# Two recurrent layers re-timed slot by slot, and an attention loop with fewer, larger transfers

## The chip, the cores and the metric

The program runs on one core of a Trainium2 chip. It is one launch, and the time is the device time of that launch in microseconds, the median of the runs. Five engines work side by side: TensorE (PE, with PEld for its weight loads), VectorE (DVE), ScalarE (ACT), GpSimd (POOL) and SyncE (SP), which here issues every transfer. Each has its own instruction stream, and they meet at semaphores.

## The reference, cut to what matters

Two blocks, each with modulated layer norms, a mixer and a feed-forward part with rounding to four bits. The mixer of the first block is attention with relative positions, 8 batches of 1024 tokens and 16 heads of 16 columns; that of the second is two recurrent layers of 512 channels and 16 states:

```python
# block 0: attention, per batch and head
scores = Q @ K.T * scale + take(Q @ pos_key.T, clip(rel)) + take(K @ pos_query.T, clip(-rel)).T
ctx = softmax(scores) @ V

# block 1: one recurrent layer (twice)
conv = causal_conv4(xc) + cb;  u = silu(conv)
dt, Bm, Cm = split(u @ xp_w.T)
dt = softplus(dt @ dt_w.T + dt_b)              # 512 channels
h_t = exp(dt_t * A) * h_(t-1) + (dt_t * u_t) * B_t     # 16 states a channel
y_t = sum_n h_t[n] * C_t[n]
y = (y + u * Dskip) * silu(z)
out = layer_norm(y @ out_w.T) * ln_w + ln_b + residual
```

## The kernel before, in words

**Attention** (`attention_loop`). There are 128 heads (8 batches by 16). A head has 8 tiles of 128 queries; each engine runs a loop over pairs of heads, with the 16 tiles of a pair written out. Index `n` is the head, `i` the tile, `m = 8n + i`. In iteration `i` TensorE computes the scores of the next tile (`scores`), two position tables of the same tile index of the next head (`table`, one for each side), turns the probabilities of this tile (`turn`) and multiplies those of the tile before with the values (`context`). ScalarE copies each table from PSUM to `tab` (L966) and takes the exponent (L971); VectorE adds the near positions and takes the row maximum (L1018, L1020).

The tables are shifted row by row through memory: SP stores each `tab[:, e, :]` to `table_dram` (`store_table`, L784), and `load_skew` (L793) reads it back with a row pitch one shorter, into `skew`. A head has four parts of two tiles (`PARTS`), and each part is read with four transfers after its stores have landed. `scores` of tile 0 waits for part 0, tile 1 for part 1, tile 3 for part 2 and tile 5 for part 3. SP's program order is written out by hand in `head`: T stands for the stores of one tile, S for the reads of a part, O for `load_opnd` (three transfers: q, kl, kr, L771), E for `load_eopnd` (two transfers, L775). Over one head it is O E T0 S3 val T1 T2 S0 ctx T3 T4 S1 T5 T6 S2 T7. S0 to S2 are those of the next head, S3 the last part of this one. `eopnd` holds the first 96 rows of q and kl once more, for `table` alone.

**Recurrent layers** (`mamba_layer`, `mb_` names). A layer has 16 items of 512 tokens. An item has 64 slots: slot `s` is channel group `c = s // 16` and state `n = s % 16`. In each slot ScalarE makes `dA` (exp, ring of 2, L2198), GpSimd makes `bx = dtu * B` (ring of 4, L1921), VectorE scans `hs` (L2016) and multiplies the state of the slot before with C (`g`, L1976), and TensorE adds `g` into `y_ps` (L2159). In 18 of the 64 slots (`TIMES_C_POOL`, slots 3, 7, 10, 14, ... 60, 63) GpSimd makes `g` instead (L1928), three slots later. The rest of the next item's and the last item's work is hung on fixed slots by the `AT_` constants (L1588 to L1606). ScalarE may be at most two slots ahead of the scan and GpSimd four.

The work that the change moves: for each of the four channel groups a softplus, of six ScalarE steps in one slot (`log_steps`, L2177 to L2184), one VectorE step (`softplus_sum`, L2002) and three GpSimd steps in one slot (`make_dtu`: `rest` L1934, `dt` L1937, `dtu` L1940); the centring of the output rows on ScalarE (`center`, L2188, four instructions), their multiplication with the norm weight and addition of its bias on VectorE (L2040, L2044; in the second layer also L2049 and L2053) and the residual on GpSimd (L1952); in the first layer the same for the input rows (L2065, L2068). `silu` of `u` stands in slot 45 on ScalarE, `silu` of `z` in slot 12, each with a table load on both sides. The loops run over pairs of items, an item with `u = 1` first.

## Time and profile before

| | us |
|---|---|
| median of 3 runs | 10254.26 (10250.23 to 10259.6) |
| profiled execution, its own time | 10262.97 |
| span of the profiled execution | 10261.3 |
| attention loop | about 660 to 4070 |
| recurrent layers | about 4980 to 7270 and 7330 to 9600 |

The page divides the span by engine: PE 8391.0 us (82%), DVE 8398.0 (82%), ACT 5633.4 (55%), POOL 4948.9 (48%), and the one transfer queue 44.7%. These are means over stages with different limits, so each stage is to be read by itself.

### The profile page before, as it was taken

The page shows a single profiled execution, that of the slowest core. Times are in us where ns is not written, and L with a number is a line of the kernel's source. Part 1 is how long each engine was busy: PE and PEld are TensorE (multiplying, and loading weights), DVE is VectorE, ACT ScalarE, POOL GpSimd, SP SyncE. Part 2 cuts the span into 40 slices and gives each one's busy share as a digit, 9 for nine tenths or more (in the row PEclk, how much of TensorE's full clock was granted, in tenths as well). Part 3 has the DMA queues.
Part 4 walks back from the last instruction along what each step waited for, and adds up shares of the span by engine and source line. Part 5 has one row for each costly group of instructions (what it writes and reads, how often), then busy time and mean ns, then how long its engine had stood idle before and what let it go on. Part 6 is the DMA issues. An engine that isn't in the chain of part 4 may idle for free. (4 is left out here: it accounts for less than half of the span.)

```text
span 10261.3 us, 177062 instructions
## 1 busy us (share of the span) xinstructions
PE 8391.0 (82%) x48396; PEld 4841.9 (47%) x48396; DVE 8398.0 (82%) x13204; ACT 5633.4 (55%) x9153; POOL 4948.9 (48%) x4685
## 2 busy tenths in 40 slices
PE   4569899989988888499688888888688888887599
PEld 2236666666666666366333333333233333333366
DVE  4558888888888887699588888888688888888799
ACT  1237777777777776133365555555455555555233
POOL 0000000000000000088488888888598888888487
PEclk7779999999999999699898998898899999999799
DMA  5578888888888888311111111111122221122111
GB/s 178 204 234 281 277 278 279 279 279 278 277 279 277 277 278 261 111 43 42 61 74 76 76 68 55 68 74 75 51 80 84 84 84 71 62 81 80 45 43 40
DMA packets 1218155, 1498.79 MB, mean 146 GB/s; under 512 B 101997, under 2 KB 1073277, under 8 KB 1185000
## 3 DMA queue, kind: packets, MB, share of 16 engines
q1 hardware_dynamic: 1217832, 1495.78, 44.7%
q14 instruction: 279, 2.29, 0.1%
q8 instruction: 44, 0.72, 0.0%
HBM read 932.33 MB, written 564.60 MB: 146 GB/s over the span
## 5 line engine op out<-in xcount | busy, mean ns | idle before, releaser
L2159 PE MATMUL mb_y_ps<-mb_g,ident 128*128 128x512 f32 x4096 | 2227.9, 654 | 589.9 <-DVE mb_g L1976 356.3
L1921 POOL TENSOR_TENSOR mb_bx<-mb_dtu,mb_bc 128x512 f32<-128x512 f32 x2048 | 2569.3, 1282 | 132.7 <-DVE mb_hs L2016 78.6
L2198 ACT ACTIVATE mb_dA<-mb_dt,mb_a_neg 128x512 f32<-128x512 f32 x2048 | 1403.7, 689 | 1854.9 <-DVE mb_hs L2016 1181.4
L1355 POOL MEMSET f_magic<- 128x1 f32 x2 | 0.2, 98 | 3842.8 <-POOLq L127 3842.8
L2159 PEld LDWEIGHTS mb_y_ps<-mb_g,ident 128*128 128x128 f32 x4096 | 789.3, 204 | 1782.9 <-issue 755.4
L966 ACT ACTIVATE at_tab<-at_e_ps 128x384 f32<-128x384 f32 x2064 | 1011.8, 490 | 968.4 <-PE at_e_ps L883 967.4
L1020 DVE TENSOR_REDUCE at_nmax<-at_s_ps 128x1 f32<-128x1024 f32 x1025 | 1255.2, 1225 | 35.2
L899 PE MATMUL at_pT_ps<-ident,at_probs 128*128 128x128 f32 x8192 | 1115.7, 280 | 140.3 <-ACT at_probs L971 131.8
L971 ACT ACTIVATE at_probs<-at_s_ps,at_nmax 128x1024 f32<-128x1024 f32 x1025 | 1140.6, 1113 | 96.2 <-DVE at_nmax L1020 77.0
L899 PEld LDWEIGHTS at_pT_ps<-ident,at_probs 128*128 128x128 f32 x8192 | 920.0, 142 | 403.3 <-ACT at_probs L971 378.1
L2016 DVE TENSOR_TENSOR_SCAN mb_hs<-mb_dA,mb_carry,mb_bx 128x512 f32<-128x512 f32 x736 | 927.7, 1280 | 204.8 <-POOL mb_bx L1921 117.2
L1976 DVE TENSOR_TENSOR mb_g<-mb_hs,mb_bc 128x512 f32<-128x512 f32 x1472 | 994.0, 675 | 69.9 <-PE mb_y_ps L2159 68.6
L2016 DVE TENSOR_TENSOR_SCAN mb_hs<-mb_dA,mb_bx 128x512 f32<-128x512 f32 x736 | 893.6, 1223 | 165.0 <-ACT mb_dA L2198 96.1
L866 PE MATMUL at_s_ps<-at_opnd 105*128 105x512 bf16 (+3 forms) x2818 | 808.8, 327 | 201.9 <-DMA at_skew<-at_tables 199.2
L1018 DVE TENSOR_TENSOR at_s_ps<-at_s_ps,at_skew 128x384 f32<-128x384 f32 (+1 forms) x1025 | 541.2, 528 | 495.6 <-PE at_s_ps L870 375.1
L1928 POOL TENSOR_TENSOR mb_g<-mb_hs_sb,mb_bc 128x512 f32<-128x512 f32 x576 | 736.5, 1279 | 312.6 <-DVE mb_hs_sb L2016 180.2
L1025 DVE COPY at_probsT<-at_pT_ps 128x512 f32<-128x512 f32 x1024 | 697.0, 681 | 0.0
L918 PE MATMUL at_c_ps<-at_probsT,at_val 128*32 128x128 f32 x16384 | 663.9, 280 | 1.6 <-ACT at_probsT L978 1.6
L870 PE MATMUL at_s_ps<-ident,at_skew 128*128 128x128 f32 x2818 | 612.9, 275 | 0.0
L2092 PE MATMUL mb_ring<-mb_xc,mb_diag 128*128 128x512 f32 x1024 | 526.8, 600 | 41.6 <-ACT mb_u L2249 39.0
L918 PEld LDWEIGHTS at_c_ps<-at_probsT,at_val 128*32 128x32 f32 x16384 | 387.4, 109 | 214.6 <-issue 203.9
L866 PEld LDWEIGHTS at_s_ps<-at_opnd 105*128 105x128 bf16 x2818 | 242.8, 98 | 435.2 <-DMA at_skew<-at_tables 223.9
(236 smaller groups left out, 14473.1 us busy)
## 6 DMA issues: line engine op xcount, KB each, us to landing
at_tables<-at_tab SPq DMA_DIRECT2D x2064, 192.0 KB, 3.5
at_skew<-at_tables SPq DMA_DIRECT2D x1030, 256.0 KB, 3.1
mb_bc<-mb_bc_rows SPq DMA_DIRECT2D x256, 1024.0 KB, 6.4
at_skew<-at_tables SPq DMA_DIRECT2D x773, 128.0 KB, 3.5
at_opnd<-at_q_st SPq DMA_DIRECT2D x129, 210.0 KB, 3.4
at_opnd<-at_kl_st SPq DMA_DIRECT2D x129, 210.0 KB, 3.9
at_opnd<-at_kr_st SPq DMA_DIRECT2D x129, 210.0 KB, 5.2
at_eopnd<-at_q_st SPq DMA_DIRECT2D x130, 192.0 KB, 4.3
```

The lines of the kernel that those rows point to most:

```text
L866: mm = nc.tensor.matmul(s_ps[:, b, a * P:z * P], opnd[:, u, 0, q], opnd[:, u, side, a * P:z * P], start=True, stop=(len(near) == 0))
L899: mm = nc.tensor.transpose(pT_ps[:, hb, k * P:(k + 1) * P], probs[:, i % 2, c:c + P], ident[:, :])
L918: mm = nc.tensor.matmul(c_ps[lane * VW:(lane + 1) * VW, q:q + P], val[:, h.u, k + lane, :], probsT[:, i0 % 2, (k + lane) * P:(k + lane + 1 ...
L966: nc.scalar.activation(tab[:, e, :], e_ps[:, 0:BAND], ACT.Copy).then_inc(s_tab, 1)
L971: nc.scalar.activation(probs[:, i % 2, :], s_ps[:, i % 2, :], ACT.Exp, bias=nmax[:, i % 2:i % 2 + 1], scale=1.0).then_inc(s_exp, 1)
L1020: nc.vector.tensor_reduce(nmax[:, b:b + 1], s_ps[:, b, :], axis=AX.X, op=ALU.max, negate=True).then_inc(s_max, 1)
L1921: pool.tensor_tensor(bx[:, s % RINGS, :], dtu[:, c, :], bc[:, 0, n, :], ALU.mult).then_inc(s_bx, 1)
L1928: pool.tensor_tensor(g[:, s1 % RINGS, :], state(s1), bc[:, 1, s1 % STATE, :], ALU.mult).then_inc(s_gp, 1)
L1976: nc.vector.tensor_tensor(g[:, s1 % RINGS, :], state(s1), bc[:, 1, n, :], ALU.mult).then_inc(s_g, 1)
L2016: nc.vector.tensor_tensor_scan(state(s), dA[:, s % DA_RING, :], bx[:, s % RINGS, :], initial=carry[:, s:s + 1] if k.u else 0.0, op0=ALU.mu ...
L2159: nc.tensor.matmul(y_ps[:, c % 2, :], ident[:, :], g[:, s1 % RINGS, :], start=False, stop=(n == STATE - 1)).then_inc(s_y, 1)
L2198: nc.scalar.activation(dA[:, s % DA_RING, :], dt[:, c, :], ACT.Exp, scale=a_neg[:, c, n:n + 1]).then_inc(s_dA, 1)
```

## The change

In attention `eopnd` is gone: `table` reads the first 96 rows of `opnd`, each of whose three transfers now has its own semaphores, and `opnd` of head n+2 is loaded in iteration 6 of head n. The two table stores of a tile become one. The order on SP is now T0 S3 T1 T2 val ctx S0 T3 T4 S1 T5 O T6 S2 T7.

In the recurrent layers the softplus is split over two slots on ScalarE and three on GpSimd, the centring over two slots, and the norm steps, the residual and some others move to other slots.

```diff
-        eopnd = sb("eopnd", [ROWS, 2, 2, T], BF16)
...
-                    sp.dma_start(opnd[:, u, k, :], st[bass.ds(n, 1), :, :].rearrange("a r t -> (a r) t")).then_inc(s_op[u], 16)
-
-            def load_eopnd(n, u):
-                for k, st in enumerate((q_st, kl_st)):
-                    sp.dma_start(eopnd[:, u, k, :], st[bass.ds(n, 1), 0:ROWS, :].rearrange("a r t -> (a r) t")).then_inc(s_eop[u], 16)
+                    sp.dma_start(opnd[:, u, k, :],
+                                 st[bass.ds(n, 1), :, :].rearrange("a r t -> (a r) t")).then_inc(s_op[k][u], 16)
...
-            def store_table(n1, u1, e):
-                ge(sp, s_tab, n1 * NE + e + 1)
-                part = e // 2 // (TT // len(PARTS))
-                sp.dma_start(table_dram[u1, e % 2, e // 2, 0:P, SPAN:SPAN + BAND], tab[:, e, :]).then_inc(s_tw[part], 16)
+            def store_tables(n1, u1, t):
+                ge(sp, s_tab, n1 * NE + 2 * t + 2)
+                part = [t < z for _, z in PARTS].index(True)
+                sp.dma_start(table_dram[u1, :, t, 0:P, SPAN:SPAN + BAND].rearrange("s p u -> p s u"),
+                             tab[:, 2 * t:2 * t + 2, :]).then_inc(s_tw[part], 16)
...
-                load_opnd(n + 1, 1 - u)
-                ge(sp, s_E, (n + 1) * NE)
-                load_eopnd(n + 2, u)
                 for i in range(TT):
-                    for e in range(2 * i, 2 * i + 2):
-                        store_table(n + 1, 1 - u, e)
                     for part, (_, z) in enumerate(PARTS):
-                        if z - 1 + LAG - 1 == i + 1:
+                        if z + 1 == i:
                             load_skew(n + 1, 1 - u, part)
-                        if z - 1 + LAG - 1 == i + 1 + TT:
+                        if z + 1 == i + TT:
                             load_skew(n, u, part)
-                    if i == 0:
+                    if i == TT - 2:
+                        ge(sp, s_S, n * TT + TT)
+                        load_opnd(n + 2, u)
+                    store_tables(n + 1, 1 - u, i)
+                    if i == 2:
                         ge(sp, s_pv, n * TT)
                         load_val(n + 1, 1 - u)
...
-                if e == 0:
-                    ge(pe, s_eop[u1], h.j * 32 + 32)
+                if e < 2:
+                    ge(pe, s_op[e][u1], h.j * 16 + 16)
...
-AT_DTK, AT_DTK_ACT = (52, 2, 15, 32), (58, 8, 21, 38)
-AT_DTK_DVE, AT_DTK_POOL = (59, 9, 22, 39), (63, 13, 26, 43)
+AT_DTK, AT_DTK_ACT = (52, 2, 15, 32), (56, 8, 21, 38)
+AT_DTK_DVE, AT_DTK_POOL = (58, 11, 23, 40), (59, 12, 24, 41)
...
-AT_ONORM = 26
-AT_RES = 44
-AT_OCENTER, AT_OSCALE = 34, 37
-AT_HCENTER, AT_HSCALE = 56, 59
-AT_XIN = 48
-AT_LN = 50
+AT_ONORM, AT_OCENTER, AT_OSCALE = 26, (33, 34), 44
+AT_RES, AT_RES_LAST = 47, 50
+AT_XIN = 50
+AT_LN, AT_HCENTER, AT_HSCALE = 53, (58, 59), 61
...
-                    if scan and s in AT_DTK_POOL[1:]:
-                        make_dtu(k, AT_DTK_POOL.index(s))
+                    for i, step in enumerate((rest, make_dt, make_dtu)):
+                        if scan and s - i in AT_DTK_POOL[1:]:
+                            step(k, AT_DTK_POOL.index(s - i))
+                        if head and s - i == AT_DTK_POOL[0]:
+                            step(k.plus(1), 0)
...
-                        if s == AT_HSCALE + 2:
+                        if s == AT_HSCALE + 1:
...
                     if scan and s in AT_DTK_ACT[1:]:
-                        log_steps(k, AT_DTK_ACT.index(s), 0)
+                        exp_steps(k, AT_DTK_ACT.index(s), 0)
+                    if scan and s - 1 in AT_DTK_ACT[1:]:
+                        log_steps(k, AT_DTK_ACT.index(s - 1))
```

`exp_steps` holds the first three of the six ScalarE steps (v, abs, exp), `log_steps` the last three (p1, q1, ln). The channel groups of the `AT_DTK` tuples are 0 to 3 in order; group 0 is that of the next item.

## Rows read from the trace of the kernel before

**Rows 1.** Busy time by stretch: stretch, its length, busy of each engine, clock, DMA share, GB/s

```profile
660.00:4070.00 3410.00, 3072.57 (x34290) 2257.05 (x34292) 2777.05 (x4096) 2422.89 (x3840) 0.00 (x0) 0.99 0.88 278
4980.00:7270.00 2290.00, 1875.57 (x4096) 790.88 (x4096) 1983.46 (x2762) 1311.06 (x2052) 1966.16 (x1651) 0.90 0.18 68
```

**Rows 2.** Groups of instructions, 1500 to 3500 us: one row maximum a tile

```profile
L1020 DVE TENSOR_REDUCE at_nmax<-at_s_ps 128x1 f32<-128x1024 f32 x602 | 737.2, 1225 | 20.7
```

**Rows 3.** Waits, 1500 to 3500 us: us in total, times, longest

```profile
PE at_s_ps L866 <- DMA at_skew<-at_tables: 111.1, 80, 2.5
PE at_pT_ps L899 <- ACT at_probs L971: 77.7, 249, 0.3
```

**Rows 4.** Waits of SP's queue, 1500 to 3500 us

```profile
SPq L793 <- DMA at_tables<-at_tab: 480.3, 226, 3.7
```

**Rows 5.** The page's DMA issues: count, KB each, median us to landing

```profile
at_tables<-at_tab SPq DMA_DIRECT2D x2064, 192.0 KB, 3.5
at_opnd<-at_q_st SPq DMA_DIRECT2D x129, 210.0 KB, 3.4
at_eopnd<-at_kl_st SPq DMA_DIRECT2D x130, 192.0 KB, 5.1
```

**Rows 6.** Timeline of one head boundary: start us, us, what [idle before <-releaser]

```profile
2022.28 0.84 SPq L784 DMA_DIRECT2D at_tables<-at_tab  x2
2023.17 2.44 SPq L793 DMA_DIRECT2D at_skew<-at_tables  x4
...
2029.88 0.45 PE L866 MATMUL at_s_ps<-at_opnd 105*128 105x512 bf16 x2 [1.64 <-DMA at_skew<-at_tables]
```

**Rows 7.** Busy by stretch again, two stretches of 2 us within that head

```profile
2031.00:2033.00 2.00, 2.00 (x29) 1.40 (x28) 1.97 (x3) 1.18 (x3) 0.00 (x0) 1.00 0.34 55
2035.00:2037.00 2.00, 2.00 (x29) 1.62 (x28) 1.49 (x4) 1.73 (x3) 0.00 (x0) 1.00 1.02 370
```

**Rows 8.** Timeline of an item of the first recurrent layer, slots 8 to 13

```profile
6444.40 0.67 ACT L2177 ACTIVATE mb_v<-mb_ring,mb_cols 128x512 f32<-128x512 f32 x1
6447.73 0.61 ACT L2184 ACTIVATE mb_lnp<-mb_p 128x512 f32<-128x512 f32 x1
6449.10 1.23 DVE L2016 TENSOR_TENSOR_SCAN mb_hs<-mb_dA,mb_bx 128x512 f32<-128x512 f32 x1 [1.76 <-ACT mb_dA L2198]
6459.51 1.23 DVE L2016 TENSOR_TENSOR_SCAN mb_hs<-mb_dA,mb_bx 128x512 f32<-128x512 f32 x1 [2.55 <-ACT mb_dA L2198]
```

**Rows 9.** The same item, slots 37 and 38

```profile
6506.79 0.68 DVE L1976 TENSOR_TENSOR mb_g<-mb_hs,mb_bc 128x512 f32<-128x512 f32 x1
6507.39 4.83 DVE L2040 TENSOR_TENSOR mb_o_sb<-mb_o_sb,mb_ln 128x1024 f32<-128x1024 f32 x1
6507.39 3.74 POOL L1921 TENSOR_TENSOR mb_bx<-mb_dtu,mb_bc 128x512 f32<-128x512 f32 x3
6514.52 1.27 DVE L2044 TENSOR_TENSOR mb_o_sb<-mb_o_sb,mb_ln 128x1024 f32<-128x1024 f32 x1
```

**Rows 10.** The same item, slots 44 to 46

```profile
6525.10 2.35 POOL L1952 TENSOR_TENSOR mb_o_sb<-mb_o_sb,mb_xin 128x1024 f32<-128x1024 f32 x1
6525.25 1.23 DVE L2016 TENSOR_TENSOR_SCAN mb_hs<-mb_dA,mb_bx 128x512 f32<-128x512 f32 x1 [0.51 <-POOL mb_bx L1921]
6528.78 1.23 DVE L2016 TENSOR_TENSOR_SCAN mb_hs<-mb_dA,mb_bx 128x512 f32<-128x512 f32 x1 [1.66 <-POOL mb_bx L1921]
```

**Rows 11.** One line over both layers: min/median/max ns

```profile
L2049 DVE TENSOR_TENSOR mb_o_sb<-mb_o_sb,mb_xin x16: 1224/2281/2284, 7566.0 to 9557.0; 128x1024 f32<-128x1024 f32 x16
```

**Rows 12.** The same item, slot 59 and the passage to the next item

```profile
6555.97 1.23 DVE L2016 TENSOR_TENSOR_SCAN mb_hs<-mb_dA,mb_bx 128x512 f32<-128x512 f32 x1 [1.77 <-ACT mb_dA L2198]
6561.70 1.27 POOL L1928 TENSOR_TENSOR mb_g<-mb_hs_sb,mb_bc 128x512 f32<-128x512 f32 x1 [2.90 <-DVE mb_hs_sb L2016]
6572.07 3.70 POOL L1921 TENSOR_TENSOR mb_bx<-mb_dtu,mb_bc 128x512 f32<-128x512 f32 x3 [4.27 <-issue]
6573.44 1.29 DVE L2016 TENSOR_TENSOR_SCAN mb_hs<-mb_dA,mb_carry,mb_bx 128x512 f32<-128x512 f32 x1 [4.61 <-POOL mb_bx L1921]
```

More of the change, by code:

```diff
@@ L743, in attention_loop @@
         c_ps = pb("c_ps", [P, BANK])
-        s_op = [sem(f"opnd_loaded{u}") for u in range(2)]
-        s_eop = [sem(f"eopnd_loaded{u}") for u in range(2)]
+        s_op = [[sem(f"{n}_loaded{u}") for u in range(2)] for n in ("q", "kl", "kr")]
         s_val = [sem(f"val_loaded{u}") for u in range(2)]
@@ L837, in _ @@
                 ge(sp, s_ctx[u], 16 * (heads // 2))
-            ge(sp, s_op[0], 48 * (heads // 2 + 1))
+            for k in range(3):
+                for u in range(2):
+                    ge(sp, s_op[k][u], 16 * (heads // 2 + 1))
             ge(sp, s_val[0], 16 * (heads // 2 + 1))
-            for u in range(2):
-                ge(sp, s_eop[u], 32 * (heads // 2 + 1))
+            for part, (a, z) in enumerate(PARTS):
+                ge(sp, s_tw[part], 16 * (z - a) * (heads + 1))
             for part in range(len(PARTS)):
@@ L1946, in body @@
                         norm_scale(t, 1, s_ors)
-                    if tail and s == AT_RES:
+                    if tail and s == (AT_RES_LAST if last else AT_RES):
                         t = k.plus(-1)
@@ L1957, in body @@
                         norm_scale(t, 0, s_hrs)
-                    if head and s == AT_DTK_POOL[0]:
-                        make_dtu(k.plus(1), 0)
             run(pool, body)
@@ L2169, in body, with exp_steps @@
                 b, a = k.plus(-1), k.plus(1)
-                def log_steps(t, c, rel):
+                def exp_steps(t, c, rel):
                     m = t.n * IC + c
@@ L2179, in log_steps, with center @@
                     act.wait_ge(s_dpc, m + 1)
-                    step = Steps(act, s_achain, m * 2)
-                    step(nc.scalar.activation(e[:, :], e[:, :], ACT.Exp, scale=-1.0))
-                    step(nc.scalar.activation(p1[:, :], e[:, :], ACT.Identity, bias=one[:, :]))
+                    nc.scalar.activation(e[:, :], e[:, :], ACT.Exp, scale=-1.0).then_inc(s_achain, 1)
+                def log_steps(t, c):
+                    m = t.n * IC + c
+                    act.wait_ge(s_achain, m * 2 + 1)
+                    nc.scalar.activation(p1[:, :], e[:, :], ACT.Identity, bias=one[:, :]).then_inc(s_achain, 1)
+                    act.wait_ge(s_achain, m * 2 + 2)
                     nc.scalar.activation(q1[:, :], p1[:, :], ACT.Identity, bias=minus_one[:, :])
                     nc.scalar.activation(lnp[:, :], p1[:, :], ACT.Ln).then_inc(s_ln, 1)
-                def center(x, side):
-                    for i in range(QT):
+                def center(x, side, half):
+                    for i in range(half * rows, half * rows + rows):
                         ins = nc.scalar.activation(x[:, i, :], x[:, i, :], ACT.Identity, bias=shift[:, side, i:i + 1],
@@ L2261, in body @@
                     if head and s == AT_DTK_ACT[0]:
-                        log_steps(a, 0, 1)
-                    if tail and s == AT_OCENTER:
+                        exp_steps(a, 0, 1)
+                    if head and s == AT_DTK_ACT[0] + 1:
+                        log_steps(a, 0)
+                    if tail and s in AT_OCENTER:
+                        half = AT_OCENTER.index(s)
                         act.wait_ge(s_ors, b.n + 1)
-                        center(o_sb, 1).then_inc(s_ocen, 1)
-                    if ahead and first and s == AT_HCENTER:
-                        t = k.plus(2)
+                        center(o_sb, 1, half).then_inc(s_ocen, 1)
+                    if ahead and first and s in AT_HCENTER:
+                        t, half = k.plus(2), AT_HCENTER.index(s)
                         act.wait_ge(s_hrs, t.n + 1)
-                        center(src, 0).then_inc(s_hcen, 1)
+                        center(src, 0, half).then_inc(s_hcen, 1)
             run(act, body)
```

28 lines of the change are left out of this document (14 added, 14 removed).

## The prediction

> **What bounds the kernel now.** I read the busy time by stretch first. In attention TensorE is busy 90% (3072.6 of 3410 us), VectorE 81%, and the transfers 88% at 278 GB/s [rows 1]. In the first recurrent layer VectorE and GpSimd are both busy 86% to 87% (1983 and 1966 of 2290 us) and no other engine is near its limit by itself [rows 1]; the second does the same work. So attention is a TensorE loop with gaps, and a recurrent item is two engines interlocked: 2290 / 16 is about 143 us an item with the filling of the pipeline, and VectorE and GpSimd have about 124 and 123 us of work in it.
>
> The waits of attention come next. 602 row maxima in 2000 us are 3.32 us a tile, 26.6 us a head, 75 heads [rows 2]. Among TensorE's waits one line waits for a transfer, the scores for `skew`: 111.1 us, that is 1.48 us a head, and the other large one is for the exponent, 77.7 us or 1.03 a head, never more than 0.3 at a time [rows 3]. The timeline shows where the first lies: once a head, at the scores of tile 5, which need part 3. SP gets to T0 at 2022.28 and to S3 at 2023.17; the data are there 6.7 us later, at 2029.88, after a stall of 1.64 [rows 6]. Ahead of S3 in the queue stand five operand loads. The transfers as such are not at their limit: two neighbouring stretches carried 370 and 55 GB/s [rows 7]. It is the order and the lag of SP that hurt: it stands 480.3 us, 6.4 us a head, waiting for stores to land before it may read a part [rows 4].
>
> For the recurrent layers I followed one item through the timeline and asked at each gap of VectorE who ended it. Five places matter: slot 9 (1.76 us, ScalarE's softplus), slot 13 (2.55, silu of z) [rows 8], slot 37, where a multiplication that otherwise takes 1.2 to 1.3 us takes 4.83 beside three `bx` of GpSimd back to back [rows 9], slots 44 and 45 (0.51 and 1.66, GpSimd's three dt steps and the residual of 2.35) [rows 10], and slots 59 and 64 (1.77, 4.61) [rows 12].
>
> **Attention, part by part.** A head moved 16 stores of 192 KB, operands of 3 x 210 KB and 2 x 192 KB more for `eopnd` [rows 5], skews and small ones, 7.40 MB in all (278 GB/s x 26.6 us). The change takes off 0.39 MB and ten of 39 issues. At about 0.45 us an issue (0.84 for two stores, 2.44 for four reads [rows 6]) SP's own work falls from 18 to about 13 us a head. S3 no longer stands behind O and E. The five issues ahead of it took 5 x 0.45 = 2.3 us of SP and 1.01 MB of the queue, 3.6 us at 278 GB/s; without them it goes out 2 to 4 us earlier, which is more than the stall of 1.48 us. Only the sequence O and the removal do this: stores and skew reads keep their order, and the reads were in four parts before.
>
> What is late next? Part 2: O now stands before T6 and S2, three issues of 0.4 us and 0.63 MB (2.3 us at 278 GB/s) ahead of it. S2 is issued in iteration 7 and needed three tiles later, 10 us; with 2 us to issue and 3.5 to land [rows 5] some 4 us are spare. The q operand: issued after the last scores in iteration 6, needed by the first table of the next head, two tiles less the scores or about 5.8 us later; its landing took 3.4, and a kl load behind four others 5.1 with one table more to spare [rows 5]. Both fit, q with about 2 us to spare. The new wait of SP on the scores holds up T6, whose tables come later anyway: nothing. The merged store may land later than one of 192 KB; S waits for a store one iteration old, so up to 3 us of it cost nothing, but a part read right behind it would. At 25.1 us a head the rate is 7.01 MB / 25.1 = 279 GB/s, as now.
>
> TensorE's stall also gave the exponent time to catch up. Without it I give back one more wait of 0.3 us a head [rows 3] (bounds 0 and 1.1). Attention: 128 x (1.48 - 0.3) = 150 us; bounds 190 and 50.
>
> **Recurrent layers, part by part.** *Softplus split on ScalarE, slots 8 and 9.* The six steps run from 6444.40 to 6448.34, 3.9 us [rows 8]. But ScalarE runs without a gap from there through the xc copies to the silu of slot 12: the same instructions in the same time, so the scan of slot 13 comes when it came. The stall moves, 0 gained. VectorE's own softplus step, now in slot 11, falls into a stall either way. Bounds -0.5 and +1.3. Slots 21 and 22: the GpSimd chain that ends in slot 26 does not change, 0.
>
> *Norm weight from slot 37 to 44, beside the silu of 45.* The 4.83 us contain 3.6 of waiting for GpSimd; L2049 waits 1.06 (2.28 against 1.22 [rows 11]). In slots 41 to 43 GpSimd now has three steps of 1.27 between its `bx`; by the same rates (a scan 1.23 and a product 0.68 on VectorE, 1.25 each on GpSimd [rows 9, 10]) it is 1.4 us late at slot 44. While ScalarE does its table loads and silu, 4.5 us, VectorE has the norm steps to do, which hides that. There the multiplication meets a GpSimd that is behind and so has two to four instructions ready: it waits between 0.7 (it gets in behind the first) and 4.3 us (behind all). The residual in slot 47 waits for the bias and costs 0.7 more. First layer: lost now 3.6 + 0.5 + 1.7 = 5.8; then 1.4 + 0.7 + 0.7 = 2.8 to 1.4 + 4.3 + 0.7 = 6.4. Gain -0.6 to 3.0; I take 2.5, nearer the case in which VectorE gets in after one instruction, as L2049 does, whose median and longest are both 2.28 [rows 11]. Second layer, four such steps: lost now 5.8 + 1.1 = 6.9, then the same 2.8 with 1 us for each of the three others, 5.8, up to 8.4 when all go badly: gain -1.5 to 1.1, I take 0.3.
>
> The Trainium skill, "SBUF — State Buffer", section "SBUF: two separate sides", says that a VectorE instruction with two SBUF inputs and a GpSimd one share a lock, held for the whole instruction, and that the other blocks fully. The trace agrees: 4.83 us against 1.27. The rule speaks against this change, since it says nothing of a fair turn; it is the third rival.
>
> *End of an item.* GpSimd idled 2.90 us before the `g` of slot 63, then ran `rest`, `dt`, `dtu` (3.9 us) and, at the turn of the loop, stood 4.27 us on nothing the profile shows; VectorE waited 4.61 for the first `bx` [rows 12]. With the steps in 59 to 61 they fall into the idle time, except that `dt` must await VectorE's step in slot 58, and that one ScalarE. I get the last `g` 1.2 us after its scan and the chain 1.5 us shorter; in the first layer, whose h scaling moves too, 2.2 at the turn of the loop and 0.9 otherwise, mean 1.6. Bounds 0 and 2.9. The turn of the loop remains. ScalarE's stall at 59 (1.77) moves to 58 (about 1.3) and is inside this sum.
>
> Sum: 16 x (2.5 + 1.6) + 16 x (0.3 + 1.5) = 66 + 29 = 95 us. Bounds: -30 to 230.
>
> **Sum.** 150 + 95 = 245 us off the profiled execution's 10262.97 gives 10018. That execution is 8.7 above the median, so the forecast is 10009, I say 10010.
>
> **Rivals.** *A, the attention stall is replaced.* The exponent, part 2 or the merged store takes its place. For it: the exponent is already waited for in four tiles of ten (249 of 602 [rows 2, 3]), and S waits for landings. Against: no single wait for it exceeds 0.3. Then attention gives 30, total 125: 10130. Chance 0.12.
>
> *B, the recurrent layers give nothing.* VectorE's and GpSimd's work is 124 and 123 us, and what is moved is only moved. Attention alone: 10254 - 150 = 10104. Chance 0.15.
>
> *C, slower: VectorE loses the turn to GpSimd each time.* Place: the norm steps of slots 44 to 47 and 61, 62, now beside a GpSimd that is behind. Price: 5 us instead of 1.3 to 2.3 for each of four steps in either layer, +10 in the second and +6 in the first, 256 us; with 150 from attention the time is 10360. It decides from a loss of 4.7 us an item (150 / 32). Rows 9 are for it, rows 11 against. Chance 0.05.
>
> *D, everything gives.* The stalls of slots 9, 45, 59 and 64 all vanish (7 us an item, 225) and the 190 of attention: 9840. Against: the chains above. Chance 0.13.
>
> *E, the change does not do what it says* (the stall of part 3 stays, or the q load is late by as much): 10160 to 10260. Chance 0.07, a third of it within 0.2%. The forecast case has 0.48.
>
> The range runs from 9880, well into D, to 10170, past A and B. A measurement of this kernel tells about 0.2% from no change, 20 us. Faster 0.89, same 0.05, slower 0.06.
>
> **What would show it.** TensorE's wait for `skew` near 0 and 25.3 us a head; SP's wait for stores well below 6.4 a head; no wait of the tables for `opnd`. L2040 at 1.3 to 2.6 us; the scan of slot 0 waiting about 3 us in every other item; slot 13 unchanged; items of the first layer 4, of the second 2 us shorter. It is wrong if TensorE waits for ScalarE 1 us a head more, or if L2040 stays at 5.

## The result, and the profile after

The changed kernel takes 9791.38 us (median; 9788.27 to 9793.81) where the kernel before takes 10252.24 beside it: a ratio of 0.955, 95% interval 0.9533 to 0.9566. That is 461 us less. I had forecast 245 less, 10010 us with a range down to 9880: the sign was right and the size far too small. All runs here are in the same, fast state. An interval of a ratio is about 16 us to either side, and most kernels below were run at different times than the changed one, so a difference of 17 to 25 us between two of them is near the edge of what can be told, although their single runs don't overlap. The profiled execution has a span of 9791.9 us.

Where did it go? In the trace of before the first row maximum starts at 661.2 and the last at 4066.7 us, and the scans run from 5047.9 to 9533.9. The same rows of after:

```profile
L1015 DVE TENSOR_REDUCE at_nmax<-at_s_ps x1025: 1223/1224/1226, 661.3 to 3852.9; 128x1 f32<-128x1024 f32 x171
L2014 DVE TENSOR_TENSOR_SCAN mb_hs<-mb_dA,mb_bx x736: 1193/1221/1232, 4829.3 to 8940.9; 128x512 f32<-128x512 f32 x184
L2014 DVE TENSOR_TENSOR_SCAN mb_hs<-mb_dA,mb_carry,mb_bx x736: 1252/1280/1294, 4956.0 to 9065.3; 128x512 f32<-128x512 f32 x184
```

These are one line's instructions, with the shortest, median and longest in ns and the first and last start. Attention is 213.9 us shorter (24.93 us a head instead of 26.61), the scans 4236.0 long instead of 4486.0, so 250 shorter. I had given attention 150 and the recurrent layers 95.

The waits of attention, 1500 to 3500 us, answer to [rows 3] and [rows 4]; they are us in total, times, longest. TensorE first, then SP's queue:

```profile
PE at_pT_ps L894 <- ACT at_probs L966: 51.4, 161, 0.3
PE at_e_ps L878 <- DMA at_opnd<-at_q_st: 4.4, 10, 0.7
...
SPq L788 <- DMA at_tables<-at_tab: 568.9, 317, 4.2
SPq L778 <- ACT at_tab L961: 219.8, 287, 2.0
```

The wait for `skew` is gone, and that for the exponent has not grown by what I gave back but fallen, from 77.7 to 51.4 us. Over the whole loop TensorE waits 8.3 us for `skew` where it waited 199.2. SP waits for stores more than before (568.9 against 480.3), not less: with fewer issues of its own it arrives earlier, and nobody waits for it. TensorE's busy share of the attention loop is 96% now (3074.3 of 3190 us; 90% in [rows 1]), and the transfers run at 281 GB/s where they ran at 278:

```profile
660.00:3850.00 3190.00, 3074.27 (x34232) 2221.81 (x34231) 2779.18 (x4090) 2400.01 (x3834) 0.00 (x0) 1.00 0.88 281
```

The merged store lands later than the single one of [rows 5], the q operand too:

```profile
at_tables<-at_tab SPq DMA_DIRECT2D x1032, 384.0 KB, 4.0
at_opnd<-at_q_st SPq DMA_DIRECT2D x130, 210.0 KB, 4.6
```

VectorE's waits over all scans, before (first four lines) and after:

```profile
DVE mb_hs L2016 <- POOL mb_bx L1921: 181.4, 146, 6.3
DVE mb_hs L2016 <- ACT mb_dA L2198: 178.8, 110, 2.6
DVE mb_g L1976 <- PE mb_y_ps L2159: 68.6, 85, 2.7
DVE mb_hs_sb L2016 <- ACT mb_dA L2198: 26.9, 18, 1.6
...
DVE mb_hs L2014 <- POOL mb_bx L1914: 68.9, 95, 5.3
DVE mb_hs L2014 <- ACT mb_dA L2201: 67.1, 91, 2.0
DVE mb_g L1974 <- PE mb_y_ps L2157: 38.7, 67, 2.7
DVE mb_hs L2014 <- issue: 20.6, 6, 4.1
```

Waits for GpSimd's `bx` on `mb_hs` fell by 112 us (181.4 to 68.9), and those for ScalarE's `dA` by as much (178.8 to 67.1): the latter is what my forecast had at nearly nothing. VectorE's busy time over the scans is unchanged, 3922.7 us before and 3919.1 after, but what it holds is not. Beside GpSimd an instruction's time contains waiting, so I read the busy time and mean ns of the norm weight and of the softplus step, before (first two lines) and after:

```profile
L2040 DVE TENSOR_TENSOR mb_o_sb<-mb_o_sb,mb_ln 128x1024 f32<-128x1024 f32 x32 | 139.6, 4362 | 7.6 <-ACT mb_o_sb L2188 7.6
L2002 DVE SCALAR_TENSOR_TENSOR mb_v<-mb_v,mb_lnp 128x512 f32<-128x512 f32 x128 | 143.0, 1117 | 54.1 <-ACT mb_lnp L2184 54.1
...
L2038 DVE TENSOR_TENSOR mb_o_sb<-mb_o_sb,mb_ln 128x1024 f32<-128x1024 f32 x32 | 51.5, 1609 | 7.6 <-ACT mb_o_sb L2191 7.6
L2000 DVE SCALAR_TENSOR_TENSOR mb_v<-mb_v,mb_lnp 128x512 f32<-128x512 f32 x128 | 220.1, 1720 | 55.8 <-ACT mb_lnp L2187 55.8
```

The norm weight gave 88 us, and the softplus steps took 77 of them. The slots of an item, as in [rows 8] to [rows 12]:

```profile
6154.08 1.22 DVE L2000 SCALAR_TENSOR_TENSOR mb_v<-mb_v,mb_lnp 128x512 f32<-128x512 f32 x1
6158.48 1.23 DVE L2014 TENSOR_TENSOR_SCAN mb_hs<-mb_dA,mb_bx 128x512 f32<-128x512 f32 x1 [1.41 <-ACT mb_dA L2201]
...
6218.95 1.27 POOL L1921 TENSOR_TENSOR mb_g<-mb_hs_sb,mb_bc 128x512 f32<-128x512 f32 x1
6219.66 1.64 DVE L2038 TENSOR_TENSOR mb_o_sb<-mb_o_sb,mb_ln 128x1024 f32<-128x1024 f32 x1
6220.18 3.48 POOL L1914 TENSOR_TENSOR mb_bx<-mb_dtu,mb_bc 128x512 f32<-128x512 f32 x2
6223.01 1.72 DVE L2042 TENSOR_TENSOR mb_o_sb<-mb_o_sb,mb_ln 128x1024 f32<-128x1024 f32 x1
...
6260.08 4.70 POOL L1914 TENSOR_TENSOR mb_bx<-mb_dtu,mb_bc 128x512 f32<-128x512 f32 x3
6264.63 1.29 DVE L2014 TENSOR_TENSOR_SCAN mb_hs<-mb_dA,mb_carry,mb_bx 128x512 f32<-128x512 f32 x1 [1.64 <-issue]
...
8167.35 1.29 DVE L2014 TENSOR_TENSOR_SCAN mb_hs<-mb_dA,mb_carry,mb_bx 128x512 f32<-128x512 f32 x1 [4.06 <-issue]
```

Slot 9 has no wait any more (slot 10 now has one of 0.88 for `bx`), and slot 13 waits 1.41 instead of 2.55 (2.00 in the item before this one). The norm weight takes 1.64 us in slot 44, where it took 4.83 in slot 37. At the turn of the loop VectorE stands 1.64 us (4.61 before), and on nothing that the profile shows (`issue`): GpSimd, which stood 4.27 us there, runs through. The last line is a turn in the second layer, where VectorE still stands 4.06 us. The waits at the first scan of an item, summed over all items but the first of each layer, fell from 75.3 to 27.3 us; the ten turns among them fell from 53.9 to 27.3. An item became 8.2 us shorter in the first layer (139.1 to 130.9) and 8.3 in the second (137.8 to 129.5).

### The profile page after: what moved, and what is told of

The parts are those of the page before. It is cut to its first block and busy times, and to the rows that moved or that the text cites. A ratio compares the mean times of both kernels' runs of the same rounds, so it can differ in the third digit from the quotient of the medians.

```text
span 9791.9 us, 174268 instructions
## 1 busy us (share of the span) xinstructions
PE 8306.5 (85%) x48396; PEld 4746.0 (48%) x48396; DVE 8402.3 (86%) x13204; ACT 5594.2 (57%) x9153; POOL 4993.0 (51%) x4685
## 5 line engine op out<-in xcount | busy, mean ns | idle before, releaser
L1914 POOL TENSOR_TENSOR mb_bx<-mb_dtu,mb_bc 128x512 f32<-128x512 f32 x2048 | 2662.0, 1324 | 9.8 <-DVE mb_hs L2014 9.7
L2157 PE MATMUL mb_y_ps<-mb_g,ident 128*128 128x512 f32 x4096 | 2196.5, 643 | 461.2 <-DVE mb_g L1974 237.7
L2157 PEld LDWEIGHTS mb_y_ps<-mb_g,ident 128*128 128x128 f32 x4096 | 765.2, 199 | 1646.7 <-issue 726.3
L894 PE MATMUL at_pT_ps<-ident,at_probs 128*128 128x128 f32 x8192 | 1115.7, 279 | 100.3 <-ACT at_probs L966 81.4
L894 PEld LDWEIGHTS at_pT_ps<-ident,at_probs 128*128 128x128 f32 x8192 | 894.7, 141 | 402.2 <-ACT at_probs L966 373.4
L1974 DVE TENSOR_TENSOR mb_g<-mb_hs,mb_bc 128x512 f32<-128x512 f32 x1472 | 992.8, 674 | 40.1 <-PE mb_y_ps L2157 38.7
L865 PEld LDWEIGHTS at_s_ps<-ident,at_skew 128*128 128x128 f32 x2818 | 392.5, 142 | 85.1 <-issue 0.4
```

The lines of the kernel that those rows point to most:

```text
L865: mm = nc.tensor.matmul(s_ps[:, b, kt * P:(kt + 1) * P], skew[:, u, 1, kt, blk * P:(blk + 1) * P], ident[:, :], start=False, stop=(kt == n ...
L894: mm = nc.tensor.transpose(pT_ps[:, hb, k * P:(k + 1) * P], probs[:, i % 2, c:c + P], ident[:, :])
L1914: pool.tensor_tensor(bx[:, s % RINGS, :], dtu[:, c, :], bc[:, 0, n, :], ALU.mult).then_inc(s_bx, 1)
L1974: nc.vector.tensor_tensor(g[:, s1 % RINGS, :], state(s1), bc[:, 1, n, :], ALU.mult).then_inc(s_g, 1)
L2157: nc.tensor.matmul(y_ps[:, c % 2, :], ident[:, :], g[:, s1 % RINGS, :], start=False, stop=(n == STATE - 1)).then_inc(s_y, 1)
```

## The experiments

### The two halves

`attn_only` is the attention loop of after with the recurrent layers of before; `rec_only` the reverse.

> The changed attention loop with the recurrent layers of before. The two traces put 214 us of the 461 into attention (last row maximum at 3852.9 instead of 4066.7 us). If the two halves are independent, this takes 214 us off: about 10038. If the halves share a cost (the transfer queue, the clock), it differs from 10038 by over 20 us.

> The changed recurrent layers with the attention loop of before. The traces put 250 us there (scans from 5047.9 to 9533.9 before, 4829.3 to 9065.3 after). Independent halves: about 10005. Otherwise off by over 20 us.

Measured: 10045.15 (0.9793, interval 0.9776 to 0.9809), 210 us less, and 10001.4 (0.9751, 0.9735 to 0.9767), 254 less. Together 464 against 461: the halves add. Both exceed their forecast, attention by 60 and the recurrent layers by 159.

### Attention: the store or the operands

`merge_only` is the kernel before with one store a tile:

```diff
-                sp.dma_start(table_dram[u1, e % 2, e // 2, 0:P, SPAN:SPAN + BAND], tab[:, e, :]).then_inc(s_tw[part], 16)
+                sp.dma_start(table_dram[u1, :, t, 0:P, SPAN:SPAN + BAND].rearrange("s p u -> p s u"),
+                             tab[:, 2 * t:2 * t + 2, :]).then_inc(s_tw[part], 16)
```

`oper_only` is the reverse: the operands loaded in iteration 6, no `eopnd`, SP's new order, but two stores a tile.

> Before with one change: the two table stores of a tile are one. Theory A, the order of the queue (operand loads ahead of the reads of part 3) makes the stall: the merge alone gives at most 30 us. Theory B, SP's own work (39 issues a head at 0.45 us) makes it late and so the stall: eight issues less are 3.6 us a head, the wait for skew falls by more than half and 100 us or more go.

> Before with the other half of attention's change: the second copy of the operands is not loaded, the three operand loads stand in iteration 6, two stores a tile as before. Theory A: 190 to 214 us less, about 10045. Theory B: about half of it, 10150.

Measured: 10219.94 (0.9967, 0.9954 to 0.9979), 35 us less, and 10057.03 (0.9806, 0.9789 to 0.9822), 198 less. In `merge_only` TensorE still waits 171 us of 199 for `skew`; in `oper_only` that wait is gone. Theory B, SP's own work, is out: eight issues fewer a head leave most of the wait. Theory A fits, though the merge gave a little more than the 30 us that it allowed (22 to 47 by the interval). With the operands moved, the merged store adds 12 us (10057 to 10045).

### Attention: their bytes or their place

`attn_bytes` puts the two loads of `eopnd` back behind `load_opnd` in iteration 6, into a buffer that nothing reads:

```diff
                         load_opnd(n + 2, u)
+                        load_eopnd(n + 2, u, h.j + 1)
```

> The changed kernel with the two loads of 192 KB each that the change took away put back, at the change's own place (behind the operand loads in iteration 6, from the same memory into a buffer that nothing reads). Theory (it is the place of the loads ahead of the reads of part 3 that cost, not their bytes): 9791 to 9815 us, TensorE's wait for skew stays below 20 us in 2000 us of attention, the rate in GB/s rises by 5% to about 295. Rival (the transfers are near their limit, so that 0.39 MB of 7.4 MB a head are worth their share): 0.39 MB at 281 GB/s are 1.4 us a head, so about 9970, with TensorE waiting for skew or opnd again.

Measured: 10097.29 (0.9852, 0.9836 to 0.9869). Contrary to what its expectation says, this kernel has the recurrent layers of before, so its base is `attn_only`, 10045: the loads cost 52 us, and by the row maxima attention is 60 us longer. Neither theory is right as put: the first allowed 24 us, the rival asked for 179. The rate went up to 292 GB/s (282 in `attn_only`, both from 1500 to 3500 us) and the wait for `skew` nearly stayed away, as "place" said; but the loads came back as a wait for q, 66.7 us in 104 times over the loop:

```profile
PE at_e_ps L889 <- DMA at_opnd<-at_q_st: 66.7, 104, 1.7
...
PE at_s_ps L872 <- DMA at_skew<-at_tables: 12.6, 18, 5.9
```

So of the 210 us about 52 belong to the two loads taken away, some 12 to the merged store (above), and the rest, about 146, to the place of the operand loads. It also prices a step of the forecast: q was said to have 2 us to spare. With its two extra neighbours in the queue it had none.

### VectorE's softplus step, slot 9 or 11

`dve11` is the kernel before with one constant changed:

```diff
-AT_DTK_DVE, AT_DTK_POOL = (59, 9, 22, 39), (63, 13, 26, 43)
+AT_DTK_DVE, AT_DTK_POOL = (59, 11, 22, 39), (63, 13, 26, 43)
```

> Before with one number changed: VectorE's softplus step of channel group 1 in slot 11 instead of 9. Theory A: in slot 9 it holds back the scan of slot 10, for which ScalarE waits 1.73 us before the silu of slot 12; in slot 11 it lies beside the silu, and the silu starts up to 2 us earlier: 2 us x 32 = 64 us less, about 10190. Theory B, as the prediction had it: ScalarE is busy without a gap from slot 8 to 13 and nothing is gained, 10250.

Measured: 10192.25 (0.9944, 0.9927 to 0.9961), 58 us less, 1.8 us an item. This is the step that I had at nothing. What I had overlooked stands in the trace of before, ScalarE's `dA` of slot 12 and VectorE's step in slot 9 ahead of it:

```profile
6450.89 1.35 DVE L2002 SCALAR_TENSOR_TENSOR mb_v<-mb_v,mb_lnp 128x512 f32<-128x512 f32 x1
...
6453.41 0.69 ACT L2198 ACTIVATE mb_dA<-mb_dt,mb_a_neg 128x512 f32<-128x512 f32 x1 [1.73 <-DVE mb_hs_sb L2016]
6454.11 1.28 ACT L2205 ACT_TABLE_LOAD   x1
```

ScalarE does not run through to silu. It waits 1.73 us for the scan of slot 10, since it may be only two slots ahead, and that scan stands behind VectorE's step of 1.35. The silu then starts about 1.3 us later, and slot 13 pays it: in `dve11` ScalarE's wait there is 0.47, that of slot 13 is 1.24 instead of 2.55, and all the waits for `dA` on `mb_hs` are 143.0 instead of 178.8 us. The other part of the 58 us is in VectorE's wait for `y_ps`, 43.4 instead of 68.6:

```profile
DVE mb_hs L2016 <- ACT mb_dA L2198: 143.0, 114, 1.8
DVE mb_g L1976 <- PE mb_y_ps L2159: 43.4, 65, 1.7
```

### ScalarE's six steps in one slot, GpSimd's three in one

`act_together` and `pool_together` are the changed kernel with one of its splits taken back. In the first, `log_steps` follows `exp_steps` in the same slot, for all four groups:

```diff
                         exp_steps(k, AT_DTK_ACT.index(s), 0)
-                    if scan and s - 1 in AT_DTK_ACT[1:]:
-                        log_steps(k, AT_DTK_ACT.index(s - 1))
+                        log_steps(k, AT_DTK_ACT.index(s))
```

In the second, all three steps stand where the last one stood:

```diff
-                    for i, step in enumerate((rest, make_dt, make_dtu)):
-                        if scan and s - i in AT_DTK_POOL[1:]:
+                    for step in (rest, make_dt, make_dtu):
+                        if scan and s - 2 in AT_DTK_POOL[1:]:
```

> The changed kernel with the six ScalarE steps of the softplus in one slot. Theory A: the split itself is worth the stall that is gone at slots 9, 22 and 59, 2 to 3 us an item: 60 to 100 us slower, about 9870. Theory B: the order on ScalarE does not matter as long as it has no gap: under 20 us.

> The changed kernel with GpSimd's three dt steps together in the last of their three slots. Theory A: spreading fills idle time of GpSimd and is worth 1.5 to 3.9 us an item at the passage between items and little elsewhere: 50 to 120 us slower, about 9880. Theory B: the three steps cost the same wherever they stand, as the prediction had it for slots 24 to 26: under 20 us.

Measured: 9833.49 (0.9596, 0.958 to 0.9612), 42 us more than after, and 9816.65 (0.9579, 0.9563 to 0.9595), 25 more. With the six ScalarE steps together the waits for `dA` behind them are back, in two neighbouring items 0.7 to 1.1 us behind three of the four softplus, and 1.76 at slot 9 in one of the two:

```profile
DVE mb_hs L2014 <- ACT mb_dA L2201: 145.9, 117, 2.0
DVE mb_hs L2014 <- POOL mb_bx L1914: 72.6, 99, 5.3
```

They grew from 67.1 to 145.9 us, and only 42 us reached the time. The trace has the counterweight: with the steps together VectorE's softplus steps take 148.0 us in all, where they take 220.1 in the changed kernel.

In `pool_together` it is the other way round. Its waits at the turns are shorter than after the change (17.4 against 27.3 us), and so are the norm weights (38.7 against 51.5), but VectorE's softplus steps take 284.4 us, 64 more. So what the split on GpSimd is worth shows in what VectorE's softplus step stands behind. Its 25 us lie between theory B's limit of 20 and the 50 where A begins, nearer to B.

### The norm steps in their old slots

`norm_back` is the changed kernel with the norm weight in slot 37 and the residual in slot 44:

```diff
-AT_ONORM, AT_OCENTER, AT_OSCALE = 26, (33, 34), 44
-AT_RES, AT_RES_LAST = 47, 50
+AT_ONORM, AT_OCENTER, AT_OSCALE = 26, (33, 34), 37
+AT_RES, AT_RES_LAST = 44, 44
```

> The changed kernel with the norm steps in slots 37 to 40 again and the residual in 44 (both layers). Theory A: the multiplication loses its turn to GpSimd again and the silu of 45 stands bare: 3 to 3.5 us an item, 100 us slower than the changed kernel, about 9890. Theory B: in the changed kernel GpSimd is behind at slot 37 and VectorE gets in at once, so only the bare silu costs, 1.5 us an item: about 9840.

Measured: 9873.59 (0.9632, 0.9615 to 0.9648), 82 us more. The wait of 1.67 us behind the residual, at slot 45, is back as well. The price of one norm weight went up, since behind the three `bx` GpSimd had a fourth instruction ready, `rest`:

```profile
6102.74 6.07 DVE L2038 TENSOR_TENSOR mb_o_sb<-mb_o_sb,mb_ln 128x1024 f32<-128x1024 f32 x1
...
6102.78 3.72 POOL L1914 TENSOR_TENSOR mb_bx<-mb_dtu,mb_bc 128x512 f32<-128x512 f32 x3
6106.46 1.25 POOL L1926 TENSOR_TENSOR mb_e<-mb_q,mb_e 128x512 f32<-128x512 f32 x1
```

The 6.07 us are 4.85 until about 6107.6, when GpSimd's fourth instruction ends, and 1.22 of work. Beside this L2038 of after, shown above: 1.64 us in slot 44. VectorE asks at 6219.66, GpSimd's `g` ends half a microsecond later, at 6220.2, and VectorE gets in before the next `bx`, which then takes 3.48 us for two instead of 2.5.

### What the norm weight waits for

Three kernels are the one before with the norm weight's multiplication (L2040) replaced by something that needs almost no time: `lock_tiny` by the same operation on 8 columns, `lock_none` by one with a single SBUF input, `lock_free` by the statistics instruction. The diff has the three in this order, each in its own kernel:

```diff
-                            nc.vector.tensor_tensor(o_sb[:, :, :], o_sb[:, :, :],
-                                                    ln[:, 0:1, :].to_broadcast([P, QT, D]), ALU.mult).then_inc(s_ochain, 1)
+                            nc.vector.tensor_tensor(o_sb[:, 0, 0:8], o_sb[:, 0, 0:8],
+                                                    ln[:, 0, 0:8], ALU.mult).then_inc(s_ochain, 1)
...
+                            nc.vector.tensor_scalar(o_sb[:, 0, 0:8], o_sb[:, 0, 0:8], 1.0, None,
+                                                    ALU.mult).then_inc(s_ochain, 1)
...
+                            nc.vector.bn_stats(stats[:, 1, 0, :], o_sb[:, 0, 0:8]).then_inc(s_ochain, 1)
```

> The kernel before, with the multiplication by the norm weight (L2040) left out but for 8 of its 1024 columns: an instruction of two SBUF inputs that needs almost no time by itself. Theory (what makes the 4.83 us is the wait to start beside GpSimd's instructions, whatever the size): it still takes 3.5 to 3.9 us, and the kernel gains at most 1.2 us x 32 = 38 us, so 10212 to 10250. Rival (the long instruction is slowed while it runs, in proportion to its data): it takes under 0.5 us and the kernel gains 100 us or more.

> The kernel before, with the multiplication by the norm weight (L2040) left out and in its place an instruction of 8 columns with one SBUF input instead of two. Theory (only an instruction of two SBUF inputs must wait for GpSimd): it takes 0.1 to 0.3 us, and the kernel gains what L2040 lost on the path, up to 4.5 us x 32 = 144 us, at least 60: 10106 to 10190. Rival (any instruction on SBUF is kept out): as the one with two inputs, 10212 to 10250 and 3.5 us.

> The kernel before, with the multiplication by the norm weight (L2040) left out and in its place the statistics instruction of 8 columns (the operation of L1987, which takes 0.35 us beside GpSimd everywhere in the trace: one SBUF input, a few numbers out). Theory (L2040 waits 3.6 us to start because it needs what GpSimd's instructions hold, and this operation does not): it takes 0.1 to 0.4 us. On the path that is worth at most 4.6 us x 32 = 147 us (10100), and at least the 31 us of the kernel with 8 columns and two inputs; as GpSimd was 3.7 us ahead of VectorE meanwhile, I take 60 to 147: 10100 to 10190. Rival (it stands at something else, a semaphore or the turn of slot 37): 3.7 us again and 10205 to 10225.

The same line in the three kernels, in that order:

```profile
L2040 DVE TENSOR_TENSOR mb_o_sb<-mb_o_sb,mb_ln x32: 166/3772/3802, 5248.9 to 9508.6; 128x8 f32<-128x8 f32 x32
```

```profile
L2040 DVE TENSOR_SCALAR mb_o_sb<-mb_o_sb x32: 170/3770/3795, 5252.1 to 9501.1; 128x8 f32<-128x8 f32 x32
```

```profile
L2040 DVE BATCH_NORM_STATS2 mb_stats<-mb_o_sb x32: 153/157/170, 5253.4 to 9484.1; 128x6 f32<-128x8 f32 x32
```

Measured: 10216.1 (0.9962, 0.995 to 0.9975), 10212.53 (0.9964, 0.995 to 0.9978) and 10179.72 (0.9929, 0.9912 to 0.9945): 31, 34 and 72 us less. So 3.6 of the 4.83 us have nothing to do with the work. An instruction of 8 columns pays them in full, the statistics instruction in the same slot, reading the same tile, not at all. It is a wait of certain VectorE instructions for GpSimd to be done, not one for a semaphore. My control with one input fell: it waits too. The Trainium skill, "SBUF — State Buffer", section "SBUF: two separate sides", counts instructions in a mode of two ports among those that take the lock, beside those with two SBUF inputs; that `tensor_scalar` from SBUF to SBUF runs in such a mode fits, but no run here shows the mode itself.

The time gained looks small against the instruction. From `lock_tiny` to `lock_free` L2040 falls from 100.8 to 5.1 us in all, 96 us, and the kernel gains 72 - 31 = 41. The trace of `lock_free` says where the rest went, to the next instruction of the kind that waits, the bias addition one slot later (1.27 us in `lock_tiny`, 41.1 us in all; here 106.2):

```profile
L2043 DVE TENSOR_TENSOR mb_o_sb<-mb_o_sb,mb_ln x32: 1224/3567/3590, 5255.9 to 9484.3; 128x1024 f32<-128x1024 f32 x32
```

So 65 of the 96 us were only handed on, and the 31 left are about what the time shows (36 us by the medians of the two kernels, 41 by their differences to before). Taking the wait out of one instruction does not say what the wait is worth as long as another one stands right behind it.

### The end of an item

`end_late` is the changed kernel with the first group's softplus two slots later, as before the change:

```diff
-AT_DTK, AT_DTK_ACT = (52, 2, 15, 32), (56, 8, 21, 38)
-AT_DTK_DVE, AT_DTK_POOL = (58, 11, 23, 40), (59, 12, 24, 41)
+AT_DTK, AT_DTK_ACT = (52, 2, 15, 32), (58, 8, 21, 38)
+AT_DTK_DVE, AT_DTK_POOL = (60, 11, 23, 40), (61, 12, 24, 41)
```

> The changed kernel with the softplus of the next item's first channel group two slots later: ScalarE in 58 and 59, VectorE in 60, GpSimd in 61 to 63 (the change has 56 and 57, 58, 59 to 61). Theory (the whole chain ScalarE, VectorE, GpSimd at the end of an item sets when the first bx of the next item comes, and being early is worth what the other parts do not explain, 47 us in all): 9825 to 9850 us, 1 to 1.8 us an item, with the scan of slot 0 waiting longer for bx by that much. Rival (the turn of the loop hides it, or only the split counts): 9785 to 9805.

Measured: 9808.06 (0.9566, 0.955 to 0.9582), 17 us more, 0.5 an item, between the theory and its rival. The wait for `bx` does grow, from 68.9 to 115.8 us, and that for `dA` on `mb_hs_sb` from 11.4 to 47.5; most of that is made good elsewhere, 28 us of it in the softplus steps (220.1 to 192.2) and 16 in VectorE's standing on nothing (20.6 to 4.2). GpSimd's standing at the turn is back in part, 15.3 us in 5 turns where before it was 45.6 in 10 and after none.

### Which engine is the bound now, and the turn

`pool16` is the changed kernel with 16 products with C on GpSimd instead of 18, `turn4` with four items in one turn of the loop instead of two; then both together, and 14 products with four items. The first part of the diff is `pool16`, the second `turn4`:

```diff
-TIMES_C_POOL = tuple(s for s in range(IC * STATE) if s * 18 // (IC * STATE) != (s + 1) * 18 // (IC * STATE))
+TIMES_C_POOL = tuple(s for s in range(IC * STATE) if s * 16 // (IC * STATE) != (s + 1) * 16 // (IC * STATE))
...
-                with eng.Fori(1, items // 2 - 1) as j:
-                    body(Item(j, 1), True, True, True, True)
-                    body(Item(j + 1, 0), True, True, True, True)
+                with eng.Fori(1, items // 2 - 1, 2) as j:
+                    for i in range(2):
+                        body(Item(j + i, 1), True, True, True, True)
+                        body(Item(j + i + 1, 0), True, True, True, True)
```

> The changed kernel with 16 instead of 18 of the 64 products with C on GpSimd: GpSimd has 2 x 1.27 = 2.5 us less an item, VectorE 2 x 0.68 = 1.4 more. In the changed kernel both are busy 94% and 95% of two items. Theory (GpSimd's bx is what VectorE waits for, 77 us in both layers, and its instructions hold VectorE's up): 0 to 1 us an item shorter, 9760 to 9795. Rival (VectorE is the bound by now): 1 to 1.4 us an item longer, 9823 to 9836.

> The changed kernel with four items instead of two in one turn of the recurrent loop, so that three turns of six remain in each layer. Theory (at the turn GpSimd stands about 4.3 us on nothing that the profile shows, and VectorE waits for it): 6 turns fewer, 3 to 4.5 us each, 18 to 27 us: 9764 to 9773. Rival (the longer body costs as much again in fetched instructions, or the stall is only moved): 9785 to 9800.

> The changed kernel with 16 of the products with C on GpSimd and four items a turn: both of the last two edits. Theory (they take different waits: one at every GpSimd product, one at the turn): additive, 9791 - 36 - 22 = 9733, 9725 to 9745. Rival (with GpSimd relieved the turn is hidden): 9750 to 9758.

> The same with 14 products with C on GpSimd. Theory (VectorE, 94.4% busy with 16, has the last 5% in waits for ScalarE and for y_ps that GpSimd doesn't end, so another 1.4 us an item of its own work now counts): 9735 to 9780, not faster than with 16. Rival (GpSimd's instructions still hold VectorE's up): another 20 to 36 us less, 9700 to 9715.

Measured: `pool16` 9755.27 (0.9517, 0.9501 to 0.9533), 36 us less than after; `turn4` 9768.92 (0.9529, 0.9513 to 0.9544), 22 less; both 9761.13 (0.9512, 0.9496 to 0.9527); with 14 products 9778.71 (0.9529, 0.9513 to 0.9545). The ratio of both together does not differ from that of `pool16` alone, so these two are the fastest here, 0.3% to 0.4% below the change: with GpSimd relieved the turn is mostly hidden, as the rival said (VectorE waits 10.1 us at the ten turns of `pool16`, 27.3 after). What `pool16` gains besides stands in VectorE's softplus step, whose median falls from 1.65 to 0.68 us:

```profile
L2000 DVE SCALAR_TENSOR_TENSOR mb_v<-mb_v,mb_lnp 128x512 f32<-128x512 f32 x128 | 113.5, 887 | 55.6 <-ACT mb_lnp L2187 55.6
```

That is 107 us less than after, against 43 us more for the 64 products that VectorE took over (0.68 each) and 18 us more in the norm weight (51.5 to 69.5). And 14 products are 18 us slower than 16 with the same loop. The waits of `pool14_turn4` over the scans:

```profile
DVE mb_g L1975 <- PE mb_y_ps L2158: 70.7, 89, 3.4
DVE mb_hs L2015 <- POOL mb_bx L1915: 68.8, 107, 5.3
```

Beside `pool16_turn4`, VectorE's wait for `y_ps` has gone from 49.4 to 70.7 us and the one for `bx` from 59.1 to 68.8, although GpSimd has two products fewer; GpSimd's wait for ScalarE's softplus (`lnp`) has gone from 58.2 to 105.4. So VectorE's added work counts, and the trace points to the chains through TensorE and ScalarE as what comes up in GpSimd's place.

## Why the prediction was wrong, point by point

**What bounds it.** Right: attention is TensorE with gaps, a recurrent item two interlocked engines. The five places that I listed are those where most of the recurrent time came from; VectorE's wait for `y_ps`, which I had not listed, gave another 30 us (68.6 to 38.7).

**Attention, the stall.** Right in mechanism and size. The wait for `skew` was to go, and did (199.2 us over the whole loop, 1.56 a head, to nothing that counts). That the place of the operand loads does it is shown by `oper_only` and `attn_bytes`; I gave the removed loads no value of their own, and they have 52 us. By my own terms a head was to take 25.4 us, not the 25.3 that I wrote as a sign; it takes 24.93.

**Attention, the give-back.** Here a step failed, by its sign. I wrote that the stall "gave the exponent time to catch up" and gave back 0.3 us a head. In the trace of before the opposite can be read, at each head:

```profile
2003.31 0.45 PE L866 MATMUL at_s_ps<-at_opnd 105*128 105x512 bf16 x2 [1.72 <-DMA at_skew<-at_tables]
2007.40 0.77 PE L899 MATMUL at_pT_ps<-ident,at_probs 128*128 128x128 f32 x5 [0.33 <-ACT at_probs L971]
```

The scores that come late start their maximum and exponent late, and 4.1 us after every stall TensorE waits for that exponent too: 2029.88 and 2033.97, 2056.00 and 2060.10, and so on. Over the loop these waits were 131.8 us in 421 times, and are 81.4 in 256: two a head remain, and the one that followed the stall went with it. The sum should have been (1.56 + 0.33) x 128 = 242 less a little for q (12.5 us by the waits of after), nearer to the 214 measured than 150.

**Attention, what is late next.** Right: part 2, T6 and the merged store cost nothing, q 0.1 us a head. SP's wait for stores was to fall well below 6.4 us a head and rose to 7.1, without consequence; I took a queue's idle time as a sign, which it is not.

**Softplus split on ScalarE and VectorE's step: 0.** This is the step that failed most, and the term that is missing: 58 us for VectorE's step (`dve11`) and 42 for the split (`act_together`), some 100 of the 159 that the recurrent forecast was short of (the two were measured on different kernels, so that their sum is not strict). "ScalarE runs without a gap from there through the xc copies to the silu of slot 12" was wrong. I had looked at the rows of the six steps and of the two stalls [rows 8], not at ScalarE's own row before the table load, where its 1.73 us wait for VectorE stands. The stall of slot 13 hung on no chain of ScalarE alone but on one that runs ScalarE, scan, VectorE's step, scan, ScalarE, and so it could be shortened; that of slot 9 is ScalarE's own (1.76 us in `dve11` too), and goes with the split. My own bound of +1.3 us an item held only for the split (42 / 32 = 1.3); 1.8 for VectorE's step came on top.

**GpSimd's steps one per slot.** I had them at 0 in the middle and inside the sum at the end. Taking them back costs 25 us, by the trace through VectorE's softplus step, which I had called free "either way": it is the instruction that the changed kernel made dearer, by 77 us.

**Norm weight.** The mechanism was right: it gets in behind the first of GpSimd's instructions, L2038 takes 1.64 and not 5. The term was 45 us (16 x 2.5 and 16 x 0.3); `norm_back` says 82, though with a worse old slot than the real one (6.05 against 4.83 us). The residual's stall is inside both figures. I had been too careful with the second layer, where I took 0.3 us and the four steps measured 1.64, 1.73, 1.73 and 1.21 us, and no lag of GpSimd of 1.4 us at slot 44 is seen (0.46 us of wait for `bx`). Rival C, VectorE losing each turn, needed 5 us for each.

**End of an item.** The term was 50 us. The waits at the first scan of the items fell by 48 (75.3 to 27.3 us), so its size was right by the trace, though `end_late`, which takes back only part of it, gives 17. The way was in part another. I had said that the turn of the loop remains. Only half of it did: VectorE's waits at the ten turns fell from 53.9 to 27.3 us, about 3 us each as forecast (the other passages went from 21.4 to none), and GpSimd's time on nothing there went from this row (of before) to none.

```profile
POOL mb_bx L1921 <- issue: 45.6, 10, 5.1
```

The slots bear on it: with GpSimd's steps in 61 to 63 (`end_late`) 15.3 us of it are back, with all three in 61 (`pool_together`) none. Why they free GpSimd of it is not shown; that it has a `bx` or two in hand when it reaches the end would fit. `turn4`, with six turns fewer, gains 22 us, and VectorE's waits at the turns fall there from 27.3 to 10.3 us, so VectorE's share is real.

**The sum.** 58 + 42 + 25 + 82 + 17 = 224 of the 254 us. The addends come from different kernels, one built on before and four on after, and `norm_back` has a dearer old slot, so this is a rough account and no proof. The 30 that remain are open: the centring in two slots, the loads' slots and whatever the undos share were not taken apart. By layer the miss was larger in the second: 8.3 us an item where I had 1.8, and 8.2 in the first where I had 4.1. The bounds that I gave, -30 to 230, don't follow from my terms either, which add up to -50 and 200; the measured 254 lies outside both.

**The rivals.** The result has the size of rival D, everything gives (9840), for which I had 0.13. Against it I had written only "the chains above", and the chain was the step that failed. The measured 9791 lies below D and below the range.

## What to carry to other kernels

Before a split or a shift on an engine is costed at nothing because "it runs without a gap", read that engine's own rows up to the instruction that ends the stall. A wait of 1.7 us in them means here that the chain passes through another engine, and whatever stands there ahead of the awaited instruction is on the path. Two waits that always come at a fixed distance behind each other (a stall and 4.1 us later a short one) can be one cost, as here, and go together. When an instruction's own time contains a wait, look at the next instruction of its kind before you price it. And where two engines are 94% to 95% busy, move work between them in small steps with a run for each: here 18 to 16 products gave 36 us and 16 to 14 took 18 back.

## What the runs showed of the hardware

A VectorE instruction of 8 columns can take 3.77 us beside GpSimd, as long as it is of the kind that has to wait for it (two SBUF inputs, or the one-input `tensor_scalar` on fp32), while `bn_stats` on the same tile takes 0.157. The price differs with what GpSimd has ready back to back: 3.6 us behind three `bx`, 4.8 behind four instructions, 0.4 to 0.5 where GpSimd changed from a `g` to a `bx`. But VectorE does not always have to let a row of `bx` pass. In the changed kernel the input rows' multiplication (1.22 us by itself) gets in between two of them, and the two then take 3.46 us instead of 2.5:

```profile
6255.44 3.46 POOL L1914 TENSOR_TENSOR mb_bx<-mb_dtu,mb_bc 128x512 f32<-128x512 f32 x2
...
6255.55 2.23 DVE L2063 TENSOR_TENSOR mb_src<-mb_src,mb_mod 128x1024 f32<-128x1024 f32 x1
```

What decides who gets the next turn is open. Other instructions pay too: VectorE's softplus step has a median of 1.65 us after the change and 1.32 before, with 0.67 as its shortest.

The turn of the loop cost GpSimd 4.6 us each of ten times before and nothing visible after, and VectorE still 0.8 to 4.1 us each. Ten turns made four gained 22 us; with GpSimd less loaded most of that was gone already, and the two together gained nothing over the lighter load alone.
